# Layer 0's edge scans: one long scan for 68 rows, one for the maxima, with ScalarE's results in PSUM

## What is computed

```python
attn = a_src_node[src] + a_dst_node[dst] + e_score
attn = jnp.where(attn >= 0, attn, NEG_SLOPE * attn)
attn_max = jnp.zeros((n, H), attn.dtype).at[dst].max(attn)
attn = jnp.exp(attn - attn_max[dst])
attn_sum = jnp.zeros((n, H), attn.dtype).at[dst].add(attn)
attn = attn / (attn_sum[dst] + EPS_SOFTMAX)
msg = h[src] * attn[:, :, None]
out = jnp.zeros((n, H, HD), h.dtype).at[dst].add(msg)
```

## Time and profile before

| | us |
|---|---|
| median of 3 runs | 4755.95 |
| the three runs | 4751.53 to 4757.55 |
| span of the profiled execution | 4755.7 |
| busy in it: GpSimd | 3565.7 |
| VectorE | 2619.7 |
| PE (matmul) | 1308.6 |
| ScalarE | 493.5 |
| moved by DMA, mean | 131 GB/s |

### The profile page before, as it was taken

The page is one execution under the profiler, slowest core; times in us unless marked ns, Lnnn a source line. Parts: engine busy times, 40 slices in busy tenths (PEclk is TensorE's granted clock), DMA queues, the critical chain, the costliest instruction groups (busy, mean ns, idle before and its releaser), DMA issues. The chain is left out here.

```text
span 4755.7 us, 33914 instructions
## 1 busy us (share of the span) xinstructions
PE 1308.6 (28%) x3363; PEld 660.9 (14%) x3363; DVE 2619.7 (55%) x8568; ACT 493.5 (10%) x1011; POOL 3565.7 (75%) x3558
## 2 busy tenths in 40 slices
PE   7600000000000000000575333333333333333336
PEld 4300000000000000000453111111111111111126
DVE  6545443344433444433774666666666666666645
ACT  4500000000000000000232111111111111111101
POOL 5777777777777777777676777777777777777766
PEclk9855555555555555555555655655665556556655
DMA  3034333333333333333232555555555555555532
GB/s 124 10 112 160 100 105 118 118 117 112 93 118 118 118 118 99 106 118 113 85 121 94 169 171 167 165 170 170 162 170 171 161 170 171 166 166 171 170 104 63
DMA packets 240932, 622.28 MB, mean 131 GB/s; under 512 B 74956, under 2 KB 102543, under 8 KB 221521
## 3 DMA queue, kind: packets, MB, share of 16 engines
q1 hardware_dynamic: 127568, 443.81, 28.2%
q0 software_dynamic: 113280, 177.74, 14.7%
HBM read 328.11 MB, written 293.29 MB: 131 GB/s over the span
## 5 line engine op out<-in xcount | busy, mean ns | idle before, releaser
L525 POOL DMA_INDIRECT edge_arena<-table1s,ix x1568 | 1518.0, 968 | 477.9 <-issue 435.2
L433 POOL DMA_INDIRECT edge_arena<-table,ix x1440 | 1460.5, 1014 | 438.9 <-issue 438.9
L565 PE MATMUL ps<-w1e_bd,edge_terms 128*128 128x512 f32 x784 | 725.1, 1080 | 1264.4 <-DMA edge_terms<-e32g_d 1264.4
L1191 DVE SCALAR_TENSOR_TENSOR edge_arena<-edge_arena,same 128x128 f32<-128x128 f32 x1568 | 542.0, 346 | 263.6 <-issue 189.1
L565 PE MATMUL ps<-we_bd,edge_terms 128*128 128x32 f32 x392 | 93.6, 403 | 1864.1 <-DVE score L1038 1803.8
L1035 DVE TENSOR_TENSOR score<-edge_arena,node_wide 128x128 f32<-128x128 f32 x49 | 14.2, 291 | 1066.0 <-DMA edge_arena<-table,ix 1065.6
L1057 DVE TENSOR_TENSOR_SCAN edge_arena<-wq,edge_arena 128x32 f32<-128x32 f32 x3136 | 586.8, 268 | 1.8
L1197 DVE SCALAR_TENSOR_TENSOR edge_arena<-edge_arena,same 128x128 f32<-128x128 f32 x1568 | 539.7, 344 | 1.5 <-ACT edge_arena L832 1.2
L565 PEld LDWEIGHTS ps<-w1e_bd,edge_terms 128*128 128x128 f32 x784 | 229.0, 322 | 1759.2 <-issue 1759.2
L1209 DVE TENSOR_TENSOR edge_arena<-edge_arena 128x1024 f32<-128x1024 f32 x196 | 240.9, 1229 | 404.5 <-DMA edge_arena<-table1s,ix 404.5
L832 ACT ACTIVATE edge_arena<-edge_arena 128x1024 f32<-128x1024 f32 x196 | 207.0, 1056 | 1800.9 <-DVE edge_arena L1214 1800.9
(11 more groups left out here) (177 smaller groups left out, 1462.5 us busy)
## 6 DMA issues: line engine op xcount, KB each, us to landing
recv_term<-zeros SPq DMA_DIRECT2D x98, 1024.0 KB, 9.1
edge_arena<-recv_term SPq DMA_DIRECT2D x196, 512.0 KB, 4.1
rows<-edge_arena SPq DMA_DIRECT2D x196, 512.0 KB, 5.1
rows<-edge_arena SPq DMA_DIRECT2D x49, 1152.0 KB, 4.4
edge_arena<-table,ix POOLq DMA_INDIRECT x1568
edge_terms<-e32g_d SPq DMA_DIRECT2D x196, 128.0 KB, 4.8
edge_arena<-table1s,ix POOLq DMA_INDIRECT x1568
edge_terms<-e16g_d SPq DMA_DIRECT2D x49, 256.0 KB, 9.2
```

The costliest lines, as they stand in the source:

```text
L433: pool.indirect_dma_start(G0[slot][:, u, :], None, table0, bass.IndirectOffsetOnAxis(ap=ix[slot][:, u:u + 1], axis=0)).then_inc(gathered0[ ...
L525: pool.indirect_dma_start(G1[slot][:, u, :], None, table1s, bass.IndirectOffsetOnAxis(ap=ix[slot][:, u:u + 1], axis=0)).then_inc(gathered1 ...
L565: return pe.matmul(out_, lhsT, rhs, start=start, stop=stop)
L1191: stt(X[:, u, :], X[:, u - 1, :] if u else Xb[:, C1 - 1, :], same[:, bass.ds(c * C1 + u, 1)], X[:, u, :], ALU.mult, ALU.add).then_inc(dv1, 1)
```

## The change

In layer 0 only. The data of a chunk is turned around: time is the innermost axis. Each of the 4 heads has 16 feature rows and one row for the sum of the weights, 68 rows in all, and each row has 33 columns: column 0 is a seed, the value at the end of the chunk before, and its multiplier is 0. So one scan over 68 x 33 = 2244 elements with start value 0 makes all rows, since at each row's start the multiplier 0 clears the state and the seed comes in. The maxima have 4 rows of 33 (`peak`), with `hold0` as multipliers and the seed in `score`.

- The product writes into a new tile `F0[par]` in place of G0, and reads the weights from PSUM (`weight`), where ScalarE writes them.
- ScalarE writes the multipliers exp(old maximum - new maximum), one for each of 17 rows a head, to PSUM (`decay`), and a second copy of the weights into F0 as the 17th row. Where a new receiver starts, VectorE has put the argument at -1000 at most (`cut`, made once from `same`), so that the multiplier is 0.
- ScalarE copies `same` into `hold0`, and after the long scan it copies F0 and `peak` into R0, from which SyncE stores as before. `rows0_ready` is now given by ScalarE.
- A slot of G0 is free after the product (`g0_free`), before after the scans.
- One-time work: `cut` (CUT is 1000.0), two cleared tiles `hold0` on GpSimd, zeroed seeds.

```diff
--- before.py
+++ after.py
@@ -166,9 +167,11 @@
         G1 = [part(edge_arena, s * W1R, C1, HID) for s in range(RING1)]
         X1 = [part(edge_arena, (RING1 + s) * W1R, C1, HID) for s in range(RING1)]
         H1 = [part(edge_arena, (2 * RING1 + s) * W1R, C1, HID) for s in range(RING1)]
-        score = sb("score", [P, C0, H])
-        expo = sb("expo", [P, C0, 2 * H])
-        wq = sb("wq", [P, C0, 2 * H])
+        T0 = C0 + 1
+        score = sb("score", [P, H, T0])
+        peak = [sb(f"peak{r}", [P, H, T0]) for r in range(2)]
+        hold0 = [sb(f"hold0_{r}", [P, H, T0]) for r in range(2)]
+        expo = sb("expo", [P, 2, H, C0])
         node_arena = sb("node_arena", [P, 13120])
@@ -204,6 +207,15 @@
         var = part(node_arena, 11706, NC)
         rstd = part(node_arena, 11716, NC)
+        HF = HD + 1
+        F0 = [part(node_arena, r * H * HF * T0, H * HF * T0) for r in range(2)]
+        F0_h = [f.rearrange("p (h d t) -> p h d t", d=HF, t=T0) for f in F0]
+        ps_flat = ps[:, :, :].rearrange("p a b -> p (a b)")
+        decay = ps_flat[:, 2 * BANK:2 * BANK + H * HF * T0]
+        decay_h = decay.rearrange("p (h d t) -> p h d t", d=HF, t=T0)
+        weight = ps[:, 7, 0:H * C0].rearrange("p (h t) -> p h t", t=C0)
+        cut = part(node_arena, 9296, LANE)
+
         big_a = part(node_arena, 4160, H, P)
         big_b = part(node_arena, 4672, H, P)
         big_c = part(node_arena, 5184, H, P)
@@ -405,6 +419,8 @@
             pool.memset(ends_i[:, 1:2], 2 * NP)
             pool.memset(ends_i[:, 2:3], -1).then_inc(cleared, 1)
             pool.memset(zeros[:, :], 0.0)
+            for r in range(2):
+                pool.memset(hold0[r][:, :, :], 0.0)
             pool.memset(upto[:, 0:1], 0.0)
             pool.memset(ones[:, :], 1.0)
             pool.memset(ident[:, :], 0.0)
@@ -465,17 +481,17 @@
             scatter_terms(0, 1)
             gather_columns(C0 + SPREAD * NK, RING0 * C0)
             pool.reg_mov(gather_turn, RING0 + 1)
-            pool.reg_mov(free_turn, 2)
+            pool.reg_mov(free_turn, 1)
             with pool.Fori(0, (K0 - 1) // RING0 - 1) as it:
                 for slot in range(RING0):
                     pool.wait_ge(nodes_ready, 1)
                     pool.wait_ge(ix0_ready, gather_turn)
-                    pool.wait_ge(rows0_ready, free_turn)
+                    pool.wait_ge(g0_free, free_turn)
                     pool.reg_add(gather_turn, gather_turn, 1)
                     pool.reg_add(free_turn, free_turn, 1)
                     gather0(slot)
             pool.wait_ge(ix0_ready, K0)
-            pool.wait_ge(rows0_ready, K0 - 3)
+            pool.wait_ge(g0_free, K0 - 4)
             gather0(0)
@@ -743,17 +759,40 @@
                                    scale=-1.0, accum_out=sign_sum[:, bass.ds(j * 2 + i, 1)]).then_inc(row_free[i], 1)
-            def turn0(c, slot, copies):
-                act.wait_ge(expo_ready, c + 1)
-                act.activation(wq[:, :, :], expo[:, :, :], ACT.Exp).then_inc(wq_ready, 1)
+            def hold(c, par):
+                act.activation(hold0[par][:, :, 1:T0], same[:, bass.ds(c * C0, C0)].unsqueeze(1).to_broadcast([P, H, C0]),
+                               ACT.Copy).then_inc(hold0_ready, 1)
+
+            def turn0(c, slot, copies, holds):
+                par = slot % 2
+                heads = lambda a: a.rearrange("p t (h d) -> p h d t", d=HD)
+                act.wait_ge(weight_arg, c + 1)
+                act.activation(weight, expo[:, 0, :, :], ACT.Exp).then_inc(weights_ready, 1)
+                act.wait_ge(rows0_ready, c + 1)
+                act.activation(F0_h[par][:, :, HD, 1:T0], expo[:, 0, :, :], ACT.Exp)
+                act.wait_ge(decay_arg, c + 1)
+                act.wait_ge(scanned0, c + 1)
+                act.activation(decay_h[:, :, :, 1:T0], expo[:, 1, :, :].unsqueeze(2).to_broadcast([P, H, HF, C0]),
+                               ACT.Exp).then_inc(decay_ready, 1)
                 if copies:
                     ix_copy(slot, bass.ds(c * C0 + RING0 * C0, C0), C0, ix0_ready)
-
+                if holds:
+                    hold(c + 2, par)
+                act.wait_ge(scanned0, c + 2)
+                act.wait_ge(rows0_stored[par], (c - par) * 8 + 16)
+                act.activation(heads(R0[par][:, :, 0:D]), F0_h[par][:, :, 0:HD, 1:T0], ACT.Copy)
+                act.activation(R0[par][:, :, ZCOL:MCOL].rearrange("p t h -> p h t"), F0_h[par][:, :, HD, 1:T0], ACT.Copy)
+                act.activation(R0[par][:, :, MCOL:ROW].rearrange("p t h -> p h t"), peak[par][:, :, 1:T0],
+                               ACT.Copy).then_inc(rows0_ready, 1)
+
+            act.wait_ge(seeds_zero, 1)
+            for par in range(2):
+                hold(par, par)
             with act.Fori(0, (K0 - 5) // RING0) as it:
                 for slot in range(RING0):
-                    turn0(it * RING0 + slot, slot, True)
+                    turn0(it * RING0 + slot, slot, True, True)
             for c in range(K0 - 5, K0):
-                turn0(c, c % RING0, c + RING0 < K0)
+                turn0(c, c % RING0, c + RING0 < K0, c + 2 < K0)
             for slot in range(RING1):
                 ix_copy(slot, slice(slot * C1, slot * C1 + C1), C1, ix1_ready)
@@ -879,7 +918,7 @@
             dve.sem_inc(x1T_mm, NPC)
             dve.sem_inc(rgT_ready, len(QUADS))
             dve.memset(end_idx[:, NB:NB + 2 * NC], 0)
-            dve.memset(R0[1][:, C0 - 1, :], 0.0).then_inc(rows0_ready, 1)
+            dve.memset(peak[1][:, :, C0:T0], 0.0).then_inc(rows0_ready, 1)
             dve.wait_ge(fused_mm, 1)
@@ -989,11 +1028,17 @@
             dve.wait_ge(onehot_ready, NK + 1)
             link(tt(same[:, 1:LANE], dst_i[:, 1:LANE], dst_i[:, 0:LANE - 1], ALU.is_equal))
             link(tt(same[:, 0:1], ends[:, 0:1], ends[:, 2:3], ALU.is_equal))
+            link(ts(cut, same[:, :], 1.0, CUT, ALU.subtract, ALU.mult))
+            link(dve.memset(F0_h[1][:, :, :, C0:T0], 0.0))
+            dve.sem_inc(scanned0, 1)
             ts(below[:, 0, :], ident[:, :], ends[:, 3:4], None, ALU.mult).then_inc(seg_mm, 1)
             dve.wait_ge(fused_mm, 2)
             stt(same_seg[:, :], ps[:, 7, 128:256], ends[:, 0:1], earlier[:, :], ALU.is_equal, ALU.mult).then_inc(seg_mm, 1)
             dve.wait_ge(fused_mm, 3)
+            dve.memset(decay_h[:, :, :, 0:1], 0.0)
             dve.tensor_copy(same_segT[:, :], ps[:, 7, 256:384]).then_inc(seg_mm, 1)
+            dve.wait_ge(seg_mm, 3)
+            dve.sem_inc(seeds_zero, 1)
             dve.wait_ge(weights1_in, 16 * WEIGHT_DMAS_1)
@@ -1026,38 +1071,41 @@
                 return ap.to_broadcast(shape)
+            STEPS_T = 5
+
             def turn0(c, slot, it):
                 par = slot % 2
-                G, R, before = G0[slot], R0[par], R0[1 - par][:, C0 - 1, :]
-                same_c = same[:, bass.ds(c * C0, C0)]
-                M = R[:, :, MCOL:ROW]
+                G, F, M, Mb = G0[slot], F0_h[par], peak[par], peak[1 - par]
+                now = score[:, :, 1:T0]
+                now_t = now.rearrange("p h t -> p t h")
                 dve.wait_ge(gathered0[slot], it * (16 * C0) + 16 * C0)
-                tt(score[:, :, :], G[:, :, D:D + H], terms[:, bass.ds(c * C0, C0), :], ALU.add).then_inc(dv0, 1)
-                dve.wait_ge(dv0, c * 4 + 1)
+                tt(now_t, G[:, :, D:D + H], terms[:, bass.ds(c * C0, C0), :], ALU.add)
+                dve.tensor_copy(score[:, :, 0:1], Mb[:, :, C0:T0]).then_inc(dv0, 1)
+                dve.wait_ge(dv0, c * STEPS_T + 1)
                 dve.wait_ge(edge_mm, c + 1)
-                tt(score[:, :, :], score[:, :, :], ps[:, par, 0:C0 * H].rearrange("p (t h) -> p t h", h=H), ALU.add).then_inc(edge_mm_free, 1)
+                tt(now_t, now_t, ps[:, par, 0:C0 * H].rearrange("p (t h) -> p t h", h=H), ALU.add).then_inc(edge_mm_free, 1)
                 dve.wait_ge(edge_mm_free, c + 3)
-                stt(score[:, :, :], score[:, :, :], SLOPE, score[:, :, :], ALU.mult, ALU.max).then_inc(dv0, 1)
-                dve.wait_ge(dv0, c * 4 + 2)
-                dve.wait_ge(rows0_stored[par], it * 32 + (16 * (slot // 2) + 16))
-                for h in range(H):
-                    last = scan(R[:, :, MCOL + h], same_c, score[:, :, h], before[:, MCOL + h:MCOL + h + 1], ALU.mult, ALU.max)
-                last.then_inc(dv0, 1)
-                dve.wait_ge(dv0, c * 4 + 3)
-                tt(expo[:, :, 0:H], score[:, :, :], M, ALU.subtract)
-                tt(expo[:, 1:C0, H:2 * H], M[:, 0:C0 - 1, :], M[:, 1:C0, :], ALU.subtract)
-                tt(expo[:, 0, H:2 * H], before[:, MCOL:ROW], M[:, 0, :], ALU.subtract).then_inc(expo_ready, 1)
-                dve.wait_ge(wq_ready, c + 1)
-                tt(wq[:, :, H:2 * H], wq[:, :, H:2 * H], wide(same_c.unsqueeze(2), [P, C0, H]), ALU.mult)
-                feats = G[:, :, 0:D].rearrange("p t (h d) -> p t h d", d=HD)
```

(27 more changed lines are left out.)

5 lines of the change are left out of this document (4 added, 1 removed).

## The result

The changed kernel takes 4645.5 us (median of 4 runs, 4641.19 to 4647.49) against 4754.67 us for the kernel before (4 runs by now); the ratio is 0.9772, with a 95% interval of 0.9758 to 0.9786. The forecast was 4649, with a range of 4640 to 4675. The profiled span is 4644.2 us, before 4755.7; the profile of before is of the slowest of its four runs (4757.55).

The account below looks back on a forecast made before the run. GpSimd, issuing one gather after another, was taken as the bound in the first half. Terms: 4755.7 - 97 (loop) - 5 (first chunks) - 5.5 (tail) + 1 (set-up) = 4649.2, forecast 4649 us, range 4640 to 4675.

Parts of the forecast that it names:

- The bound and the mechanism: Layer 0 loop: GpSimd's gathers set the time; VectorE delays them reading two SBUF tiles, not with second input in PSUM.
- The border of the rule: VectorE operations beside gathers: only those reading two tiles of SBUF were taken to delay a gather.
- Part 1: Loop of 1440 gathers: weights and multipliers in PSUM remove 100.8 us of delay, less 4 for short operations: 97 us gained.
- Part 2: First four chunks, before the loop's first gather: the gathers' excess of 5 us goes as well.
- Part 3: ScalarE's new work, some 5.7 us of a chunk's period of 40, is hidden by the gathers.
- Part 4: Stretch after the last gather: 24.2 us falls to 18.6, a gain of 5.5 us.
- Part 5: Set-up: `cut` costs a gather 0 to 1.1 us and two cleared tiles 0.2 each; together 1 us more.
- The rest: Layer 1 and the node stages keep their code and gathers and only start earlier.
- The long scan as holder: Rival: the long scan holds GpSimd although its multiplier is in PSUM; about 4855 us, chance 0.10.
- The product alone as holder: Rival: only the product still holds gathers, its PSUM operand being the second input; 4730 us, chance 0.05.
- the other cause: Rival: the gathers' excess only coincides with VectorE's work, the loop stays, only the tail gains; 4751 us, chance 0.03.

Follow-up runs that it names:

- e1: The changed kernel with the product's weights back in SBUF instead of PSUM: 4781.0 us, ratio 1.0053 to the kernel before.
- e2: The changed kernel with the long scan's multipliers back in SBUF instead of PSUM: 4825.8 us, ratio 1.0145 to the kernel before.
- e3: The kernel before, short scans and in-place product kept, with ScalarE's weights and multipliers in PSUM: 4646.6 us, ratio 0.9768.
- e9: The changed kernel, unaltered, run on a third chip: 5542.1 us, ratio 0.9824 to the kernel before on that chip.
- e4: The changed kernel with the product and ScalarE's copy of F0 walked in the order of G0 and R0: 4646.9 us, one run.
- e8: The kernel before with weights, multipliers and the four whole-lane scans' multipliers in PSUM, on a second chip: 5675.9 us, ratio 1.0066.
- e11: The kernel before with weights, multipliers and the four whole-lane scans' multipliers in PSUM, on a third chip: 5671.1 us, ratio 1.0058.
- e12: The changed kernel with both weights and long-scan multipliers in SBUF, on a third chip: 5645.8 us, ratio 1.001 to the kernel before.
- e10: The changed kernel with whole-lane scan multipliers in PSUM and the last chunk's copy shared with VectorE, third chip: 5537.7 us, ratio 0.9813.

## Why the prediction was right, step by step

- **The bound and the mechanism.** GpSimd's gathers set the time of the loop, and VectorE counted only by what it did to them. e1, e2 and e3 show the cause: the place of the second input. In the scan PSUM is the first input, in the product the second, and neither holds a gather. The prediction had rested on line 1244 for the scan and on line 1214 for the product. Line 1244 was a clear test: its four gathers start 0.3 us before its end and pass. Line 1214 was a weak one. Its gathers start in its last 0.07 to 0.20 us, where a hold adds little: line 1209, just ahead of it, reads two tiles of SBUF, and the gathers that start 0.16 to 0.20 us before its end take 0.98 to 1.01 us, those at the same place in line 1214 0.94 to 0.95. The prediction took "no gather was longer" for enough, but most gathers beside line 1209 are not longer either:

```profile
3007.22 0.94 POOL L525 DMA_INDIRECT edge_arena<-table1s,ix  x1 [0.30 <-issue]
3007.24 1.23 DVE L1209 TENSOR_TENSOR edge_arena<-edge_arena 128x1024 f32<-128x1024 f32 x1 [1.87 <-DMA edge_arena<-table1s,ix]
```

VectorE starts there when a gather's rows have landed, and on this chip that falls just after a later gather has started. This operation lets a gather through that has started; only one that starts inside the operation is held. Of the 195 that start from 0.3 us before line 1209 to 0.1 after its start, two take 1.95 and 1.99 us, and these start 0.10 and 0.06 into it. In e9, where the phase has slipped, 127 of the 148 that start inside the same operation take over 1.2 us.
- **The border of the rule** was drawn too narrowly by the prediction with "two tiles of SBUF". Line 1088 has one tile as input (and one number per partition), and all 11 gathers of before that start 0.1 us or more into its 0.88 us take 1.15 to 1.57 and end 0.81 to 0.85 after it. It doesn't let through those that have started either: six that start 0.1 to 0.4 us before it end 0.12 after it (one is the 4648.97 of the earlier trace rows). Nothing in the loop of layer 0 is of that form and length, so the sum did not suffer.
- **Part 1, the loop**: 97 us forecast, 99.2 measured. Of the 4 us left for the short operations less than 2 are there: the scan of the maxima takes 0.44 us, and the mean gather is 1 ns above the median.
- **Part 2, the first chunks**: 5 forecast, 4.0 measured; gathers beside the whole-lane scans cost what they did.
- **Part 3** held: ScalarE's 819 us are hidden by the gathers, though its copy cost twice what was taken. In the first burst VectorE waited three times for this copy, 3.5, 3.5 and 1.3 us, covered as well.
- **Part 4, after the last gather, was mis-sized**: a gain of 5.5 forecast, 2.5 measured, 21.7 us in place of 18.6. Two terms failed. The product takes 3.83 and not 2.3, and from the end of the scan to the store's issue it is 4.4 and not 2.4, since the copy takes 3.87 and not 1.91. I had kept to the short scans, which step by 72 elements and took 0.268 us; but a scan has 2.08 ns for an element, and the step's cost (1.9 ns an element in all) seems to be hidden under that: the whole-lane scans, which walk `terms` in steps of four, have 2.1 as well. The prediction's sentence on the Trainium skill and its lines of 16 bytes gave the right side: 4 us later, and it was 3.
- **Part 5**: `cut` took 0.98 us, and the transfer beside it (held already by the comparison that makes `same`) 2.68 us in place of 2.19, so it cost 0.5; the cleared tiles took 0.22 each. The stage ended 1.2 us earlier, not 1 later; such a difference lies within what runs vary.
- **The rest**, forecast as unchanged, was 4.7 us shorter. The traces of e1 to e4 have 2468.6 to 2469.4 there, e3 with the code of before. So it isn't the change's doing in this stretch; it looks as if the one profile of before was long there: its run was the slowest of four, 2.9 us above their median. No second profile tests it.
- **The rivals.** The long scan as holder needed a hold of over 2.4 us a chunk: with both inputs in SBUF it has 3.8 (e2), at a price below the 4.3 taken, and 4826 us in place of 4855. With one in PSUM it has none. The product alone as holder is out by the changed kernel's gather of 1038.82, which takes 0.94 beside it, and the other cause by e1.
- **The Trainium skill**, in SBUF — State Buffer, section "Who interferes with whom", infers that tensor_tensor does not stall a GpSimd DMA. For these indirect gathers it does: 3.54 us in place of 0.94 in e1. The section's other sentence, that two SBUF inputs collide with a GpSimd instruction that reads SBUF, is the one that the runs bear out, and they extend it to the scan, which the page does not name.

The forecast of 4649 against 4645.5 had errors of opposite sign. By the profiled spans (4649.2 against 4644.2) it had 4 us too much gain, 3 at the tail and 1 in the first chunks, and 9 too little: 2.2 in the loop, 2.2 in the set-up and 4.7 in the rest. That they nearly cancel is luck.

## What to carry to other kernels

Where GpSimd issues indirect transfers without a pause, look for gathers of unusual length and for the VectorE operation that ends 0.8 us before them (a row of usual length clears an operation only if the gather starts inside it and well before its end); an operand of it that another engine writes anyway (here ScalarE's exponentials) can go to PSUM for nothing, and that was worth 2.3% here with four lines changed. A rewrite that also shortens the other engine should be tried part by part: on one chip the kernel with the short scans and PSUM did as well, on two others its like (e8, e11) was 0.6% slower than the old kernel and only the version with few instructions gained. A new layout is paid in steps: an element that lands in a line of its own costs 0.8 to 1 ns more, which is nothing beneath other work and doubles a copy at the end of a stage.

## What the runs showed of the hardware

- A gather that is caught by a VectorE operation with two SBUF inputs ends 0.75 to 0.82 us after that operation, whatever its length (1.2 to 4.8 us) and whether product or scan. Only one is caught each time, and of two inputs in SBUF only if it starts inside. In layer 1's product of 1.23 us (line 1209 before, 1257 in the changed kernel, 1259 in e12) the latest that passes starts 0.04 us into the operation, the earliest that is held 0.05 (e12). The holds of two neighbouring operations add (e12: 3.58 and 4.60).
- A VectorE operation with one input from SBUF can hold as well: line 1088 (TENSOR_SCALAR, 0.88 us) held the 11 gathers that start 0.1 us or more into it until 0.81 to 0.85 us after it, and six that had started 0.1 to 0.4 us before it until 0.12 after it.
- Reading or writing SBUF with a step of 4 elements or more costs 0.83 ns an element more on VectorE and 0.98 on ScalarE, with no difference between 4 and 8; runs of 4 and step 2 cost under 0.1. A product of 2048 elements takes 3.83 us in place of 2.28, a copy on ScalarE 3.87 in place of an estimated 1.91.
- A copy of 1024 elements from SBUF to SBUF with such steps took 1.11 us on VectorE and 2.05 on ScalarE (e10).
- The same kernels took 19% longer on two other chips, with long operations of VectorE and ScalarE as fast as on the first, some gathers of up to 2.65 us (e9), and pauses of 1.1 us between short scans (e11); the cause is not settled.
